# Attention bodies in six double slots instead of twelve single ones

## What is computed

```python
# layer 0: attention (16 heads of 32), weights scaled per row by a coherence, plus a field term
attn = softmax(q @ k.T / sqrt(32)); mod = (1 - fi) * renormalised(attn * coh) + fi * fa
x = x + (mod @ v) @ Wout.T + bout
# layer 1: masked attention, then an RMS norm of its output with gain and shift
x = x + rmsnorm(softmax(where(mask, -inf, q @ k.T * scale)) @ v @ Wo.T) * (1 + sc) + shift
# layer 2: norm, attention, norm, gated MLP
x = x + attention(tc_rmsnorm(x)); x = x + silu(h @ gate_w.T) * (h @ hid_w.T) @ out_w.T
# layer 3: spectral gate and two quaternion products (a 4x4 mix of feature chunks)
x = x + rotate(x)
```

## Time and profile before

| | us |
|---|---|
| median of 3 runs (2985.60 to 2991.92) | 2991.61 |
| the profiled execution, its own time | 2992.51 |
| its span, first to last instruction | 2990.7 |
| mean granted TensorE clock | 0.986 of full |

### The profile page before, as it was taken

One profiled execution on the slowest core, in us unless ns is written; L12 is line 12 of the kernel. 1 busy time (PEld: TensorE's weight loads), 2 busy tenths in 40 slices (PEclk: granted clock), 3 DMA queues, 4 the chain that ended last, 5 costly groups with the idle time before them and its releaser, 6 DMA issues. The chain is left out here.

```text
span 2990.7 us, 69862 instructions
## 1 busy us (share of the span) xinstructions
PE 2902.6 (97%) x27255; PEld 2520.4 (84%) x27255; DVE 2048.1 (68%) x3640; ACT 1367.8 (46%) x2226; POOL 666.8 (22%) x563
## 2 busy tenths in 40 slices
PE   6999999999999999989999999899999999999998
PEld 5899999998888898878888888688888888888886
DVE  5788788876788888888777778654444465655554
ACT  3555545544566666656666666422222232222221
POOL 1222222221121111133222333122222221111111
PEclk8999999999999999999999999899999999999999
DMA  3444444457544444575443435411212240111101
GB/s 139 95 128 123 128 131 116 129 125 188 142 99 101 105 109 100 130 169 136 105 109 105 112 102 120 153 57 57 71 56 67 78 137 29 43 57 42 56 28 43
DMA packets 514586, 300.45 MB, mean 100 GB/s; under 512 B 411776, under 2 KB 484608, under 8 KB 513952
## 3 DMA queue, kind: packets, MB, share of 16 engines
q1 hardware_dynamic: 514464, 298.76, 37.4%
HBM read 139.31 MB, written 58.72 MB: 66 GB/s over the span
## 5 line engine op out<-in xcount | busy, mean ns | idle before, releaser
L747 PE MATMUL att_bank_a<-keep_hh,keep_wgateh 128*128 128x256 f32 x1536 | 453.1, 295 | 4.8 <-ACT att_af L913 2.3
L748 PE MATMUL att_bank_a<-keep_hh,keep_wgatel 128*128 128x256 f32 x1536 | 434.3, 283 | 0.0
L749 PE MATMUL att_bank_a<-keep_hl,keep_wgateh 128*128 128x256 f32 x1536 | 434.0, 283 | 0.0
L962 ACT ACTIVATE att_shifted<-att_shifted,keep_lift 128x512 f32<-128x512 f32 x384 | 276.6, 720 | 299.2 <-DVE att_shifted L1126 295.7
L1710 DVE TENSOR_TENSOR mlp_act_t<-mlp_bank_u,mlp_sg 128x512 f32<-128x512 f32 x128 | 88.5, 692 | 453.0 <-ACT mlp_sg L1616 449.3
L1122 DVE TENSOR_REDUCE att_top<-att_bank_s 128x4 f32<-128x512 f32 x384 | 264.1, 688 | 182.2 <-PE att_bank_s L798 180.8
L1759 POOL TENSOR_TENSOR mlp_al<-mlp_act_t,mlp_ah 128x512 fp32r<-128x512 f32 x128 | 174.9, 1367 | 870.3 <-ACT mlp_ah L1622 870.3
L1616 ACT ACTIVATE mlp_sg<-mlp_bank_g 128x512 f32<-128x512 f32 x128 | 76.6, 598 | 626.3 <-PE mlp_bank_u L1540 626.1
L957 ACT ACTIVATE att_pq<-att_shifted 128x512 f16<-128x512 f32 x384 | 241.2, 628 | 201.4 <-DMA att_pt<-att_pq 195.3
L747 PEld LDWEIGHTS att_bank_a<-keep_hh,keep_wgateh 128*128 128x128 f32 x1536 | 293.0, 191 | 16.4 <-DVE att_xres L1097 2.8
L748 PEld LDWEIGHTS att_bank_a<-keep_hh,keep_wgatel 128*128 128x128 f32 x1536 | 294.1, 191 | 0.1
(11 more groups left out here) (268 smaller groups left out, 7257.4 us busy)
## 6 DMA issues: line engine op xcount, KB each, us to landing
resid<-att_xres SPq DMA_DIRECT2D x47, 512.0 KB, 2.8
keep_xin<-resid SPq DMA_DIRECT2D x33, 512.0 KB, 3.8
mlp_res<-resid SPq DMA_DIRECT2D x32, 512.0 KB, 4.6
att_xres<-resid SPq DMA_DIRECT2D x31, 512.0 KB, 4.3
mlp_xf<-resid SPq DMA_DIRECT2D x30, 512.0 KB, 4.6
keep_xin<-in_x SPq DMA_DIRECT2D x16, 512.0 KB, 4.5
att_xres<-in_x SPq DMA_DIRECT2D x16, 512.0 KB, 3.8
keep_spare<-in_w_next SPq DMA_DIRECT2D x16, 512.0 KB, 3.9
```

The costliest lines, as they stand in the source:

```text
L747: nc.tensor.matmul(out, w_h, x_h, start=first, stop=False)
L748: nc.tensor.matmul(out, w_l, x_h, start=False, stop=False)
L749: return nc.tensor.matmul(out, w_h, x_l, start=False, stop=last)
L962: nc.scalar.activation(shifted[:, u % 2], shifted[:, u % 2], ACT.Exp, bias=k["lift"][:, 0:1], scale=SCALE).then_inc(exp_done, 1)
```

## The change

The twelve slots become six double slots on every engine. PE runs the scores of both units of a chunk in one run (24 matmuls, 256 of the 512 columns of each of the four banks used), then the weighted values of the two units two double slots back in every body of every layer, then the first and the second slot's half fills with the small jobs placed anew between them. In L1 the mask is added for both units by four matmuls of 256 columns in place of eight of 128. DVE shifts both units one behind the other, and `shift_done` of both is waited for before the next chunk's scores. ACT does exponential and high part of the two units in turn. The two low parts are at different places of the double slot. `paired` goes, and the half fills are spread anew over the slots (by layer).

The diff, cut to its core:

```diff
-        bank_s = ctx.enter_context(nc.psum_tensor("att_bank_s", [P, 4, 512], F32))[:, :, 0:P]
+        bank_s = ctx.enter_context(nc.psum_tensor("att_bank_s", [P, 4, 512], F32))[:, :, 0:NB * P]
...
-            spans = [2,2,1,1,2,2,2,2,2,2,1,1] if len(fills) == 10 else [2,2,1,1,1,2,2,1,1,1,1,1]
+            if len(fills) == 10:
+                spans = [2, 2, 1, 1, 2, 2, 2, 2, 2, 2, 1, 1]
+            else:
+                spans = [2, 2, 2, 2, 1, 1, 1, 1, 1, 1, 1, 1] if lay(i) < 2 else [2, 2, 2, 1, 2, 1, 1, 2, 1, 1, 1, 0]
...
-            def scores(i, u):
+            def scores(i, c):
+                if positive(UNITS * i + NB * c):
+                    pe.wait_ge(shift_done, UNITS * i + NB * c)
+                if c % 2 == 0:
+                    pe.wait_ge(a_free[0], a_done(i, ("k", c // 2)))
+                    pe.wait_ge(a_free[1], a_done(i, ("q", c // 2)))
...
                 if masked:
                     for h in range(4):
-                        nc.tensor.matmul(bank_s[:, h, :], k["ident_b"][:], k["mask"][:], start=True, stop=False)
+                        out = bank_s[:, h, :].rearrange("p (b j) -> p b j", b=NB)
+                        nc.tensor.matmul(out, k["ident_b"][:], bcast_mid(k["mask"][:], NB), start=True, stop=False)
+                for b in range(NB):
+                    at = slice(b * P, (b + 1) * P)
+                    for step, (q_t, k_t) in enumerate(((qh, kh), (qh, kl), (ql, kh))):
+                        for h in range(4):
...
                 mm.then_inc(s_full, 1)
```

The PE's body:

```diff
-                for s in range(SLOTS):
...
+                for s in range(0, SLOTS, 2):
                     at_last = s == 0 and isinstance(i, int) and i % G == 0
                     if at_last:
                         project_pieces(pieces[s])
                     if s < UNITS:
-                        scores(i, s)
+                        scores(i, s // NB)
                     if s >= 4:
-                        for u in ([s - 5, s - 4] if s % 2 else []) if paired(i) else [s - 4]:
+                        for u in (s - 4, s - 3):
                             weigh_values(i, u)
+                    if s == 6 and lay(i) == 0:
+                        sum_values(i, 0)
+                    if s == 10:
+                        turn_output(i, 0)
                     if not at_last:
                         project_pieces(pieces[s])
-                    if s == 11 and lay(i) == 0:
+                    if s == 0 and not (isinstance(i, int) and i == 0):
+                        turn_output(i - 1, 1)
+                    if s == 2 and lay(i) == 0:
+                        for b in range(NB):
+                            coherence(i, b)
+                    if norms(i) and s == 8:
+                        norm_sums(i)
+                    project_pieces(pieces[s + 1])
+                    if s == 10 and lay(i) == 0:
                         sum_values(i, 1)
```

The ACT's body, where `read_fills(s)` is the old loop over `readable(pieces, s)`:

```diff
+                for d in range(SLOTS // 2):
+                    s = 2 * d
+                    if d == 0:
+                        for b in range(NB):
+                            first_values(i, b)
+                    if d == 5:
+                        high_output(i, 0)
+                    read_fills(s)
+                    if d == 1 and has_x(i, 1):
+                        high_x(i + 1)
...
                     if s < UNITS:
-                        exponentials(i, s)
+                        for u in (s, s + 1):
+                            exponentials(i, u)
...
+                            high_probs(i, u)
+                    if d == 0 and positive(i):
+                        high_output(i - 1, 1)
+                    if d == 4 and norms(i):
+                        deviations(i)
+                    read_fills(s + 1)
+                    if d == 0:
                         for b in range(NB):
                             second_values(i, b)
```

The DVE's body:

```diff
+                for d in range(SLOTS // 2):
+                    s = 2 * d
+                    if s >= UNITS:
+                        normalise(i, d - 2)
+                    read_fills(s)
+                    if s < UNITS:
+                        shift_scores(i, s)
+                        if d == 0 and positive(i) and lay(i - 1) == 0:
+                            add_field(i - 1, 1)
+                        shift_scores(i, s + 1)
+                    if d == 2 and lay(i) == 0:
+                        coherence_factor(i)
+                    if 2 <= d < PAIRS:
+                        normalise(i, d - 2)
+                    if s < UNITS:
+                        low_probs(i, s)
+                    if d == 0 and positive(i):
+                        low_output(i - 1, 1)
+                    if d == 1 and lay(i) == 0:
+                        coherence_sum(i)
...
+                    if d == 5:
...
+                        low_output(i, 0)
+                    read_fills(s + 1)
+                    if s < UNITS:
+                        low_probs(i, s + 1)
```

More of the change, by code:

```diff
@@ L1030, in body, with read_fills @@
                 pieces = pieces_of(i)
[L1031 to L1037 removed]
+                def read_fills(s):
                     for fill in readable(pieces, s):
@@ L1299, in body @@
                         nc.vector.tensor_copy(tb[:], k["tanh_bias"][:, :, bass.ds(NB * (i + 1), NB)]).then_inc(tb_ready, 1)
+                    if d == 4 and piece_of(i) is not None:
+                        low_piece(piece_of(i))
+                    if d == 5 and post(i):
+                        for m in range(2):
+                            norm_add(i - 1, m)
             iterate(dve, body)
```

163 lines of the change are left out of this document (52 added, 111 removed).

## The result

The changed kernel takes 2945.11 us in the median of 4 runs (2941.3 to 2947.12), the kernel before 2990.68: a ratio of 0.9849, 95% interval 0.9832 to 0.9866. It is faster, inside the range, and 27 us slower than the 2918 forecast. The profiled execution took 2946.95, with a span of 2945.2 against 2990.7.

The account below looks back on a forecast made before the run. PE's instruction list was taken to bound each body. Score runs 64.3, weighted values 4.0, vanished waits 5.3 and 3.0, less 3 for new waits, sum to 73.6: 2992.5 to 2918.9 profiled, 2918 median; range 2898 to 2953.

Parts of the forecast that it names:

- (1): Rival: in merged score runs, the second unit enters PE's array like its own run; 25 us back, 2943; chance 0.11.
- (2): Rival: third score run waits for DVE's subtractions, PE waiting 0.8 in 32 bodies; 26 us back, 2944; chance 0.12.
- Score runs, 64.3: PE's scores: four runs of six rounds replace eight of three, saving 0.335 a pair, 64.3 us over 192 pairs.
- Weighted values, 4.0: PE's weighted values: eight runs of 20 matmuls become four of 40 in 20 bodies, saving 0.20 each, 4.0 us.
- The mask, nothing: Mask matmuls before L1's scores: 0.24 eight times becomes 0.48 four times, 1.92 either way, so no gain.
- Waits that go, 5.3 and 3.0: PE's waits for DVE ahead of slot 3's scores disappear: 5.3 us saved in L2, 3.0 in L1.
- the sign named in the prediction: In PE's timeline, no wait of `att_bank_s` for L1126 should remain in L2's bodies.
- New waits, 3 lost: PE now waits for both subtractions of a chunk; 0.1 to 0.2 a body booked in L0 and L1, 3 us lost.
- In L2 it is 12.4 against 11.8: At L2's third score run, PE arrives 12.4 us after the body's first scores, DVE at 11.8; 0.6 to spare.
- the ACT, DVE and POOL work is the same: These engines' work is unchanged and has 16% idle (DVE 34 in the new 40.5), so moves carry no price.
- The changes of layer, 0 with bounds of 8: Bodies at layer changes, where weight loads delay transposes: bursts may wait longer or less; 0, bounds -8 and +8 us.
- the fourth rival: Late transposes of low probabilities delay ACT's high part, then DVE; decides from landing 4.2; 43 us slower, 3035; chance 0.07.

## Why the prediction was right, and where its sizes were off

The direction and the main term were right. That the total fell into the range is in part luck: 2945 is the time that rivals (1) and (2) gave (2943 and 2944), and neither of them took place as described. The forecast missed 31.9 us in two places and was given back 4.3 elsewhere; the changes of layer alone lay outside the bounds put on them (20.5 against 8), and the range held them since its slow end had 26 us for a wait at the third scores that did not come.

**Score runs, 64.3.** Right. The rounds follow each other at 0.11, and steady L0, where nothing else changes, went from 41.80 to 40.59: 1.21, for 1.34 in the sum less the 0.1 to 0.2 booked for new waits, and just over the 1.2 that was named as the least. Broken runs give back 1.14 to 1.19 a body. The first rival is refuted by the fourth round. The Trainium skill, TensorE: Matmul & The Clock Gate, section "Wait — 56ns, not 53.3ns?", gives 56 ns for back-to-back matmuls of 128 columns. Taken as the step of a whole round, as the prediction tried it, that does not hold here: rounds of four with their own weight loads step by 0.11.

**Weighted values, 4.0.** Undersized: 0.09 a pair and 0.36 a body instead of 0.20, 7 us over the twenty bodies. What I didn't see is how much of the order hangs on it (2.8 us a body in L1 when it was taken apart).

**The mask, nothing.** Right: L1 took 34.32 for the forecast 34.4, with mask and broadcast operand in it.

**Waits that go, 5.3 and 3.0.** They went in L1, and no wait came in their place. In L2 0.17 a body was left while the hold was there (1.7 in ten waits), where the sign named in the prediction was none; with POOL's order changed there was none.

**New waits, 3 lost.** This is the step that failed in L2. "In L2 it is 12.4 against 11.8" counted every DVE operation at its duration of before, and looked for the wait at the third score run. It came one step earlier, at the projection that needs the bank of k, and the cause was not the number of DVE's operations but their length: moved into one burst, the low probabilities met POOL's value subtractions, and took 2.85 for 0.68. The step "the ACT, DVE and POOL work is the same" was wrong in this sense. It cost 0.9 a body, 11.4 us over the thirteen bodies against the forecast. With the meeting avoided the bodies took 32.43, for 32.6 forecast. The second rival was the right kind (a wait of 0.8, in L2), but its cause and place were others, and L0 had none of it.

**The changes of layer, 0 with bounds of 8.** Undersized, and outside its bounds: 20.5 us short of the sum's terms (8.2 and 12.3; 7.9 and 8.9 in the second profile of the changed kernel). The term priced only how much longer or shorter the bursts might wait, and a wait here also costs the clock. By the windows 14.9 of the 20.5 are idle time of PE; the 5.6 left are, as an estimate, its instructions at the lower clock. In bodies 15 to 17 the idle time is mostly merged pairs waiting for transposes (9.5 for 4.1): the fourth rival's mechanism, with landings of 4.5 to 6.1 us in body 15. The steady bodies show no such wait. In bodies 28 to 33 it is the reads of k and the norms' sums, and what makes these late is open but for the held addition, 3 us in bodies 28 and 29. The weight loads cost about what they did before.

**What was better than forecast.** Body 0 and the last body with the MLP took 6.3 us less than their share. PE's waits for the scores in body 0 went from 6.1 to 4.9 us, which is a part; the rest was not looked into.

## What to carry to other kernels

An operation keeps its duration only in its neighbourhood: when an order is rewritten, list which VectorE instructions with two SBUF inputs will run beside GpSimd's two-input ones, and price them at the time until GpSimd's operation is done, or both where a second one follows at once. Cure such a meeting by moving GpSimd's work beside VectorE's reads of PSUM, since moving the held instruction only moves the hold. And price the few irregular bodies by themselves: they have other loads and other slack, and a wait there costs the clock too.

## What the runs showed of the hardware

- A VectorE subtraction of two SBUF inputs was held by GpSimd's two-input operations, in steady L2 over two of them in a row (2.85 us for 0.68), though it started 0.08 us ahead of them in the records (1480.57 against 1480.65). Behind the start of the first of L1345's two it was held over that one alone (1.52), and the second took 1.58 for 1.13. Of eight residual additions of 128 elements two were held, by one GpSimd operation each (3.95 for 2.18 in all). VectorE's operations with one input in PSUM were not held (0.67 to 0.69).
- Beside GpSimd's TENSOR_SCALAR operations of 0.45 us, with one tensor as input, the same subtraction took 0.69 in the steady bodies and 0.83 to 0.87 in three others. Where it took 0.69, the TENSOR_SCALAR was held instead (1.00 for 0.45; 4.01 for 3.45 over eight).
- One matmul over 128 rows between two rounds of 32-row matmuls costs 0.31 us, itself included.
- In a wait of 4.38 us in body 15 the granted clock went to 1.2 GHz, and stayed there over the nine matmuls of 512 columns behind the wait: they started 0.43 apart, and the next ones, at 2.4 GHz, 0.23.
